# Causal masks of the second attention: zeroed on GpSimd after the exponential, in place of products on TensorE before it

## What is computed

```python
q = _rope(q, ROPE_THETA)
k = _rope(k, ROPE_THETA)
k = jnp.repeat(k, rep, axis=2)
v = jnp.repeat(v, rep, axis=2)
...
scores = jnp.einsum('bhqd,bhkd->bhqk', q, k) / jnp.sqrt(jnp.float32(hd))
causal = jnp.tril(jnp.ones((N, N), dtype=bool))
scores = jnp.where(causal[None, None], scores, -jnp.inf)
weight = jax.nn.softmax(scores, axis=-1)
out = jnp.einsum('bhqk,bhkd->bhqd', weight, v)
out = out.transpose(0, 2, 1, 3).reshape(B, N, D)
return out @ wo
...
x = _layernorm(x + _L0_attn_ref(x, L0_attn_wq, L0_attn_wk, L0_attn_wv, L0_attn_wo), axis=-1)
```

## Time and profile before

| | |
|---|---|
| median of 3 runs | 1834.44 us (1834.43 to 1837.12) |
| the profiled execution, its time | 1829.03 us |
| its span, first to last instruction | 1827.2 us |
| TensorE busy, of the span | 1609.3 us (88%) |
| DVE / ACT / GpSimd busy | 1171.8 / 924.6 / 544.4 us |
| second attention in the trace | from 462 to 726 us |

### The profile page before, as it was taken

How to read it: one execution, slowest core, us unless ns; L and a number is a source line. 1 busy time by engine, 2 the same in 40 slices (tenths; PEclk the granted TensorE clock), 3 DMA queues, 4 the chain that set the end, 5 groups by cost and what they waited for, 6 DMA issues and landing times. The chain is left out here.

```text
span 1827.2 us, 33299 instructions
## 1 busy us (share of the span) xinstructions
PE 1609.3 (88%) x12586; PEld 807.4 (44%) x12586; DVE 1171.8 (64%) x2012; ACT 924.6 (51%) x1624; POOL 544.4 (30%) x551
## 2 busy tenths in 40 slices
PE   3869999678899997899997999877897989999997
PEld 1523333236333333344442544444554556666564
DVE  2458899335789885799875787799442243333277
ACT  3636677425467773677763566455231343333332
POOL 1657543327000011123222212255163111111155
PEclk9979999889999998899998999899897999999999
DMA  6313321100000000466646999643061763546344
GB/s 237 107 58 60 56 51 36 24 1 2 2 2 2 2 2 24 80 123 114 116 76 201 331 356 351 211 145 113 19 126 50 247 240 110 194 157 197 117 127 138
DMA packets 175118, 210.33 MB, mean 115 GB/s; under 512 B 111610, under 2 KB 114904, under 8 KB 172784
## 3 DMA queue, kind: packets, MB, share of 16 engines
q1 hardware_dynamic: 165504, 184.87, 34.1%
q0 software_dynamic: 7344, 20.73, 4.3%
q10 hardware_dynamic: 2112, 2.62, 0.4%
HBM read 193.33 MB, written 56.40 MB: 137 GB/s over the span
## 5 line engine op out<-in xcount | busy, mean ns | idle before, releaser
L728 ACT ACTIVATE attn_prob<-attn_ps_t 128x512 f32<-128x512 f32 x576 | 312.6, 595 | 157.3 <-PE attn_ps_t L682 155.8
L752 DVE TENSOR_REDUCE attn_mx<-attn_ps_s 128x2 f32<-128x1024 f32 (+3 forms) x304 | 342.3, 1161 | 43.7 <-PE attn_ps_s L663 40.5
L2035 PE MATMUL sparse_ps_g<-wgate,sparse_xT 128*128 128x352 f16 x1128 | 185.7, 315 | 3.6 <-DVE sparse_xT L2113 3.6
L695 PE MATMUL attn_ps_o<-attn_prob,V 128*32 128x256 f32 x2304 | 175.7, 391 | 0.8 <-ACT attn_oT L736 0.8
L2035 PEld LDWEIGHTS sparse_ps_g<-wgate,sparse_xT 128*128 128x128 f16 x1128 | 105.5, 98 | 75.0 <-DVE sparse_xT L2113 24.4
L1180 PE MATMUL lin_ps_z<-arena,lin_xT 128*128 128x512 f16 x576 | 135.5, 387 | 0.9 <-DVE lin_relu L1324 0.9
L682 PE MATMUL attn_ps_t<-arena,KT 64*128 64x256 f16 x1152 | 113.0, 275 | 18.3 <-DMA arena<-attn_mT 12.5
L945 PE MATMUL ffn_ps_fc<-wfcT,ffn_xT 128*128 128x512 f16 x512 | 114.3, 382 | 14.4 <-DMA ffn_xT<-ffn_x 14.4
L955 PE MATMUL ffn_ps_y<-wprojT,ffn_hT 128*128 128x512 f16 x512 | 116.9, 388 | 7.9 <-DMA ffn_hT<-ffn_h 7.9
L2146 POOL DMA_INDIRECT xg<-x_d,token x45 | 42.5, 946 | 259.0 <-PE sparse_ps_x L2025 259.0
L663 PE MATMUL attn_ps_s<-KT,arena 64*128 64x512 f16 (+3 forms) x768 | 115.5, 336 | 2.3 <-DVE attn_mx L752 2.3
(11 more groups left out here) (294 smaller groups left out, 3103.2 us busy)
## 6 DMA issues: line engine op xcount, KB each, us to landing
wgate<-gate_d SPq DMA_DIRECT2D x47, 1408.0 KB
wdown<-down_d SPq DMA_DIRECT2D x47, 768.0 KB
lin_sp_raw<-in_L_ffn_w_gate_up_dram SPq DMA_DIRECT2D x56, 352.0 KB, 5.1
gate_d<-lin_sp_parts SPq DMA_DIRECT2D x56, 352.0 KB, 4.7
y_d<-y SPq DMA_DIRECT2D x47, 256.0 KB
down_d<-lin_sp_parts SPq DMA_DIRECT2D x42, 256.0 KB, 5.0
lin_sp_raw<-in_L_ffn_w_down_dram SPq DMA_DIRECT2D x28, 256.0 KB, 5.4
wfcT<-in_L_ffn_w_fc_dram SPq DMA_DIRECT2D x8, 512.0 KB, 4.9
```

The source lines that it names most:

```text
L695: last = pe.matmul(ps_o[32 * jj:32 * jj + 32, 256 * half:256 * half + 256], V[:, kt, 4 * jg + jj, :], prob[(2 * q + jj // 2) % 4][:, half, ...
L728: act.activation(prob[g % 4][:, par, :, :], ps_t[:, (2 * g + par) % 3, :, :], ACT.Exp, scale=HD ** -0.5).then_inc(exp_done, 1)
L752: dve.tensor_reduce(mx[x % 2][:, c, :, at:at + per], ps_s[:, 2 * (r % 2):2 * (r % 2) + 2, 0:per * n].rearrange("p e (h k) -> p e h k", k=n ...
L2035: last = pe.matmul(ps_g[u][n][rows, :], xT[u][:, a, k, rows], w, start=(k == 0 and i == 0), stop=(k == KC - 1 and i == 2), skip_group_chec ...
```

## The change

In the second attention (`selected = b == 1`) the t steps of a diagonal quad have no mask products any more; the score products start the accumulation themselves. ACT takes the exponential of all keys, future ones too, and then GpSimd sets the future keys' exponentials to zero in place, with one `affine_select` for each exponential: 4 for each unit, 64 in all, with a new semaphore `sel_done`. The v steps of a diagonal quad wait for it, where they waited for the exponentials. The masks of the s steps stay. GpSimd issues the selects where the t step stands in ORDER. `attention_order` gets the argument too: a diagonal t step costs no MASK, and its exponentials are ready SELECT = 1.0 later, one after the other. So the order of all steps of the second attention is made anew. The first attention keeps its order.

```diff
+    SELECT = 1.0
...
             masked = kt == UNITS[x][0]
-            pe = when + KEYS + 8 * MASK * masked + SWITCH * (masked or mode != "row")
+            products_only = selected or not masked
+            pe = when + KEYS + 8 * MASK * (not products_only) + SWITCH * (not products_only or mode != "row")
             for par in range(2):
...
                 exp_end[2 * nt + par] = bank[(2 * nt + par) % 3] = act
+                if selected and masked:
+                    exp_end[2 * nt + par] = pool = max(pool, act) + SELECT
...
+    selected = b == 1
+    ORDER = attention_order(selected)
...
-                            if kt == qt:
+                            if kt == qt and not selected:
                                 pe.matmul(ps_t[:, (2 * g + par) % 3].rearrange("p i (a q) -> p (i a) q", q=P), m.identb[:, :],
                                           mask_k.to_broadcast([P, 4, P]), start=True, stop=False, skip_group_check=True)
...
-                                                 start=kt != qt, stop=True, skip_group_check=True)
+                                                 start=kt != qt or selected, stop=True, skip_group_check=True)
...
-                        pe.wait_ge(exp_done, 4 * q + 3 + half)
+                        if selected and kt == qt:
+                            pe.wait_ge(sel_done, 4 * x + 3 + half)
+                        else:
+                            pe.wait_ge(exp_done, 4 * q + 3 + half)
...
                 for kind, *a in ORDER:
+                    if kind == "t" and selected:
+                        g, = a
+                        x, kt = QUADS[g // 2]
+                        for par in range(2 if kt == UNITS[x][0] else 0):
+                            pool.wait_ge(exp_done, 2 * g + par + 1)
+                            p = prob[g % 4][:, par, :, :].rearrange("p i (a q) -> p (i a) q", q=P)
+                            pool.affine_select(p, p, [[0, 4], [1, P]], ALU.is_ge, 0.0, base=0, channel_multiplier=-1).then_inc(sel_done, 1)
                     if kind == "h":
```

More of the change, by code:

```diff
@@ L485, with attention_order @@
 TWO_CHUNKS = [sum(1 for qt, _ in UNITS[:x + 1] if qt >= 4) for x in range(len(UNITS))]
-def attention_order():
+def attention_order(selected):
     PAIR, MASK, KEYS, VALUES, TURN, SWITCH, FILL = 0.22, 0.053, 0.24, 0.5, 0.45, 0.1, 0.17
@@ L505, in attention_order @@
     out = []
-    pe = dve = act = 0.0
+    pe = dve = act = pool = 0.0
+    SELECT = 1.0
     mode = None
@@ L599, in attend @@
 def attend(nc, m, d, b, QT, KT, V):
-    ORDER = attention_order()
+    selected = b == 1
+    ORDER = attention_order(selected)
     summed = {e[2]: e[1] + 1 for e in ORDER if e[0] == "c"}
@@ L629, in attend @@
         mt_in = [f.sem(f"mt_in{u}") for u in range(2)]
-        t_done, exp_done, v_done, o_evac, rec_done = f.sems("t_done exp_done v_done o_evac rec_done")
+        t_done, exp_done, sel_done, v_done, o_evac, rec_done = f.sems("t_done exp_done sel_done v_done o_evac rec_done")
         o2 = [f.sb(f"o2{u}", [P, 2, D], F16) for u in range(2)]
```

## The result

The changed kernel takes 1845.18 us (median of 14 runs, 1832.96 to 1850.71), the kernel before 1835.16 us on the same chips (14 runs, 1830.50 to 1840.07). The ratio is 1.0045, with a 95% interval of 1.0028 to 1.0062: some 10 us slower (5 to 11), where 4.4 less were forecast, and above the end of the forecast's range, 1844. The profiled execution took 1844.72 us (span 1842.9).

The account below looks back on a forecast made before the run. TensorE's busy time was taken as the bound in the scored part (462 to 672 us) and output part (672 to 717 us). -8.4 + 0.3 + 2.35 + 1.3 = -4.4 us gave 1830.0 us; range 1820 to 1844.

Parts of the forecast that it names:

- What bounds the kernel: Second attention: TensorE bounds both parts; DVE stands 23.9 us of idle time behind it in the scored part.
- What is removed: Diagonal t steps: 32 times 0.54 us of mask products, 17.3 us of TensorE time, 15.1 in the scored part.
- The price of a select: GpSimd: one select of 512 elements takes S = 0.95 us, set between bounds of 0.65 and 1.157.
- The replays: Diagonals of units 9, 10, 11 replayed in the new orders: mean gain 0.70 us, for 12 units -8.4 us.
- The wait for selects: TensorE waits about 1 us ahead of v(2q) in each diagonal; some 0.4 of 1.08 us saved goes back.
- The output part: Attention's end, 672 to 717 us: selects of units 14 and 15 queue behind roots on GpSimd, +0.3 and +2.35 us.
- The port: GpSimd's selects slow DVE's small steps on the maxima: 4 us of DVE time, +1.3 us on the path.
- The slow select: Rival: a select takes over 1.06 us and TensorE stands at the v steps: 1839 to 1851 us; chance 0.25.
- DVE takes it up: Rival: TensorE reaches s steps sooner but DVE frees slots no sooner; half the gain lost, 1834 us; chance 0.11.
- a step in the replay that isn't ready, 14 times over: Listed sign of being wrong: a replayed step not ready when let start, repeated 14 times; no size given.
- a lower clock in the new gaps: Listed sign of being wrong: a lower granted clock in TensorE's new gaps; no size given.

Follow-up runs that it names:

- e6: Changed kernel with the old order and neither mask products nor selects in the second attention's diagonals (output wrong there): 1830.81 us, ratio 0.9970.
- e1: Changed kernel, selects kept, with the order of the kernel before in both attentions: 1835.45 us, ratio 1.0001.
- e2: Kernel before, mask products kept and no selects, with the changed kernel's order in the second attention: 1846.97 us, ratio 1.0057.
- e4: Changed kernel with the planner's LANDING at 3.3 (2.4 before) and SELECT at 0.65 (1.0 before) in the second attention: 1826.69 us, ratio 0.9963.
- e8: Kernel before, with its mask products, and the planner's LANDING at 3.3 in the second attention: 1838.25 us, ratio 1.0007.
- e3: Changed kernel and its order with neither selects nor mask products in the second attention's diagonals (output wrong there): 1837.22 us, ratio 1.0014.

## Why the prediction was wrong

**What bounds the kernel:** half right. TensorE stood on the path, but the earlier trace rows were read as if its busy time bound the scored part. The chain from a unit's last reduction over the transfers to the next unit's first t step was as long in the seven units in which TensorE waited for it already before (4.4 us in all), and is not made shorter by relieving TensorE.

**What is removed:** the size was right, its worth not. 17.3 us of products were worth 3.7 (e6 against before), because waits took their place: 4.9 us more for the transfers of the maxima and 4.2 us more for DVE.

**The price of a select:** wrong, 0.95 us where 0.637 was measured. This error points the other way: by the prediction's own replay 0.65 would have given 1820 us. The lower bound, worked out from GpSimd's cast and its one-element operation, was the price. (Its slope is (296 - 194)/127 = 0.80 ns an element, not 0.83, and the bound 0.60 us, not 0.62; nothing else changes by that.) The 769 ns which the Trainium skill has (GPSIMD Engine Reference, section 3.1) are nearer than mine, and above the measured number too.

**The replays: the step that failed.** "Unit 9: [...] v58 not before 1.1 + 3S = 3.95, t60 4.52": the replay lets the next unit's first t step start when the steps ahead of it are through, and never asks when the maxima land. Put beside the timeline of the changed kernel:

| | t60 / t72 / t84 starts, replay | measured | t62 / t74 / t86, replay | measured |
|---|---|---|---|---|
| unit 9 | 4.52 | 5.19 | 6.54 | 8.01 |
| unit 10 | 2.5 | 3.17 | 5.58 | 6.25 |
| unit 11 | 4.52 | 5.21 | 6.54 | 8.04 |

These are unit 10's and unit 11's rows of TensorE:

```profile
594.67 0.39 PE L687 MATMUL attn_ps_t<-arena,KT 64*128 64x256 f16 x4
...
597.84 0.39 PE L687 MATMUL attn_ps_t<-arena,KT 64*128 64x256 f16 x4 [1.24 <-DMA arena<-attn_mT]
...
600.92 0.39 PE L687 MATMUL attn_ps_t<-arena,KT 64*128 64x256 f16 x4
```

```profile
612.77 0.38 PE L687 MATMUL attn_ps_t<-arena,KT 64*128 64x256 f16 x4
...
617.98 0.39 PE L687 MATMUL attn_ps_t<-arena,KT 64*128 64x256 f16 x4 [1.02 <-DMA arena<-attn_mT]
...
620.81 0.61 PE L687 MATMUL attn_ps_t<-arena,KT 64*128 64x256 f16 x4
```

Each of the three is late by 0.67 to 0.69 us at the landing; units 9 and 11 lose 0.8 us more behind it, at the lower clock. That the three are alike is chance: the waits for the landing are 1.08, 1.24 and 1.02 us, and at units 9 and 11 the select that was priced too dear hides a part of them. With 0.64 us for a select the replay has t60 at 3.6. Set against the kernel before as the prediction did, the measured diagonals are 1.03, 0.37 and 0.14 us longer, 0.51 in the mean, where 0.70 of gain was forecast. Times 12 that is +6.2 us; the scored part grew by 6.8. So near a hit is partly luck, since two of these three units have a fall of the clock, and in the whole scored part there are only five. But the term that turned the sign is the missing one, and the trace of before had the number for it. There t84 waited 0.80 us and started at 612.29, and DVE's transpose had begun at 608.88, in this row of the kernel before:

```profile
608.88 0.21 DVE L766 STREAM_TRANSPOSE attn_mT<-attn_top 128x32 f16<-128x32 f16 x1
```

That is 3.41 us, and so it is, 3.41 or 3.42 us, at all 19 t steps of the two kernels that wait for a landing, the first unit's left out. I read this wait as one that the selects' wait would cover, and did not carry the 3.4 us to the other units.

**The wait for selects** of about 1 us at each v(2q), with which the forecast gave back 0.4 us a unit: not there. In the scored part of the changed kernel TensorE's matmuls don't wait for the selects at all: at unit 9 the third is through 2.9 us after t58 starts, and v58 starts at 3.5.

**The output part**, +2.65 forecast, +4.8 measured: too small a term by 2.1 us. The swap alone is worth 0.8 us there with the old order (e1 against before) and 0.7 with the new (changed kernel against e2); the new order costs 4.0 (against e1), and no run shows by what alone. The mechanism that was named is in the trace:

```profile
719.58 0.55 POOL L463 TENSOR_TENSOR attn_ln_rstd<-attn_ln_var,minus_half 128x1 f32<-128x1 f32 x1 [4.92 <-DVE attn_ln_var L458]
720.09 2.40 POOL L827 TENSOR_SCALAR_AFFINE_SELECT attn_prob<-attn_prob 128x512 f32<-128x512 f32 x4
721.96 1.23 PE L703 MATMUL attn_ps_o<-attn_prob,V 128*32 128x256 f32 x16 [1.60 <-POOL attn_prob L827]
```

Unit 15's four selects stand behind the root of w step 6, and the last v steps wait 1.60 us for them.

**The port**, +1.3 on the path out of 4 us of DVE time: the mechanism is there and smaller. DVE's casts and maxima of a unit grew from 175 and 214 ns to 260 and 293, which is 8 x 0.085 + 8 x 0.079 = 1.3 us of DVE time in all. In units 0 to 14 five of them took longer than 0.18 us, up to 0.60, and each of the five ran beside a select. The reductions didn't grow: 128x2 from 128x1024 took 1217 ns before and 1216 after. By the Trainium skill (SBUF — State Buffer, "Who interferes with whom") reductions never exclude GpSimd; the trace agrees.

**The rivals.** The slow select had a time near the result and a chance of 0.25, but its mechanism is refuted. DVE takes it up: in part. TensorE's waits for a slot grew from 2.1 us to 6.3 in e6 and to 6.8 in the changed kernel, beside the larger waits for the landing, and DVE is as busy as TensorE once the order is mended (e4). What came true stood among the ways to be wrong: a step in the replay that isn't ready, 14 times over, and a lower clock in the new gaps. It should have been the rival on the slower side: the products taken away stood between a unit's maxima and the t steps that wait for them, and nothing in the change moves the landing.

## What to carry to other kernels

When a cost is taken out of a planned order, the order moves with it: run the change once with the old order and the old work once with the new order before judging either. A transfer's landing that a planner sets too low does no harm that was seen while the engine is late anyway (e8 gains nothing over before), and can cost more than the relief brings once that engine is relieved (7.8 us of the scored part here); take such constants from the trace, from the same starting point as the planner (here 3.2 us against 2.4). And a replay of an order must have a term for each wait in the code, the ones hidden so far too.

## What was not expected of the hardware

- GpSimd's affine select in place on 128x512 f32 takes 0.637 us, less than its subtraction of two inputs at the same size (1.157 us) and for an element less than half of what its comparison with a scalar operand takes (2.849 us for 1024).
- Four transfers of 1 KB each, issued within 2.11 us, are there 3.41 to 3.42 us after the start of the transpose that feeds them, in both kernels and at all 19 t steps that wait for them, the first unit's left out.
- The granted clock fell to 1.2 GHz for some microseconds after waits of 1.0 to 1.4 us in the changed kernel, five times in 190 us, while e3, with 14 waits of the same sort and 15.2 us of them, kept 2.4 GHz from 470 to 660 us; e1 and e6 show one fall each there. What tells the two apart stayed open.
